# z's products ahead of the gate's in the front of a chunk, and GpSimd's four u ahead of the first scan inputs, with a new merge table

## What is computed

```
xn   = layernorm(x)
z    = xn @ W_in;   gate = silu(xn @ W_gate)
dt   = clip(softplus(z @ W_dt + b_dt), 0.001, 1.0)
Bp   = z @ W_B;     Cp = z @ W_C;   A = -clip(exp(A_log), 1e-6, 1)
h    = exp(dt * A) * h + dt * Bp * z          # step by step over the tokens
y    = sum over states of h * Cp;   out = x + (y * gate) @ W_out
```

## Time and profile before

| what | value |
|---|---|
| median of 3 runs | 3286.13 us (3277.07 to 3286.29) |
| span of the profiled execution | 3287.9 us |
| TensorE busy | 2907.9 us, 88% |
| VectorE busy | 2739.3 us, 83% |
| ScalarE busy | 2096.2 us, 64% |
| GpSimd busy | 1925.7 us, 59% |

### The profile page before, as it was taken

How to read it: one execution, slowest core, us unless ns; L and a number is a source line. 1 busy time by engine, 2 the same in 40 slices (tenths; PEclk the granted TensorE clock), 3 DMA queues, 4 the chain that set the end, 5 groups by cost and what they waited for, 6 DMA issues and landing times.

```text
span 3287.9 us, 45422 instructions
## 1 busy us (share of the span) xinstructions
PE 2907.9 (88%) x14848; PEld 2380.8 (72%) x14848; DVE 2739.3 (83%) x4612; ACT 2096.2 (64%) x3852; POOL 1925.7 (59%) x1541
## 2 busy tenths in 40 slices
PE   6567698998999899898989989899999989998898
PEld 4455477787877778687777868777777877777676
DVE  3777989797998979799898979889897989989541
ACT  2546476676757677675767767576766767575433
POOL 1766667564766757475675756576575647666110
PEclk8558699999999999999999999999999999999998
DMA  4241123231322323232322323232232323223122
GB/s 130 96 159 39 52 81 111 92 102 64 129 82 91 125 78 100 70 118 85 100 103 81 106 79 125 66 106 92 87 109 86 108 76 121 78 71 120 56 103 76
DMA packets 152778, 308.56 MB, mean 94 GB/s; under 512 B 18368, under 2 KB 96984, under 8 KB 135136
## 3 DMA queue, kind: packets, MB, share of 16 engines
q1 hardware_dynamic: 152000, 302.52, 27.6%
q10 hardware_dynamic: 272, 1.57, 0.1%
q0 software_dynamic: 272, 1.57, 0.1%
HBM read 288.27 MB, written 17.35 MB: 93 GB/s over the span
## 4 chain that ended last, share of the span: by engine, by line
PE 48%; DVE 18%; issue 13%; ACT 12%; POOL 5%; DMA 1%; DVEq 0%; SPq 0%; POOLq 0%; ACTq 0%
PE ps_B L1870 11%; PE ps_B L1765 10%; PE ps_A L1765 8%; DVE hs L1527 8%; PE ps_H L1760 7%; DVE acc L1491 5%; PE ps_H L1778 4%; PE ps_B L1760 3%; POOL bu L1100 3%; PE ps_B L1778 3%; PE ps_B L1917 2%; ACT ps_A L1288 2%; DMA bb<-b_rows 1%; DVE hA L1719 1%; ACT acc L1300 1%
## 5 line engine op out<-in xcount | busy, mean ns | idle before, releaser
L1100 POOL TENSOR_TENSOR bu<-z,bb 128x512 f32<-128x512 f32 x1024 | 1294.2, 1290 | 289.9 <-DVE hs L1527 146.7
L1527 DVE TENSOR_TENSOR_SCAN hs<-ps_A,state,bu 128x512 f32<-128x512 f32 x768 | 976.5, 1276 | 21.7 <-ACT ps_A L1288 11.4
L1288 ACT ACTIVATE ps_A<-dt,a_neg 128x512 f32<-128x512 f32 x1024 | 699.3, 686 | 355.7 <-DVE hs L1527 351.5
L1760 PE MATMUL ps_H<-ident,hs 128*128 128x128 f32 x4096 | 652.6, 294 | 195.3 <-DVE acc L1491 123.1
L1760 PEld LDWEIGHTS ps_H<-ident,hs 128*128 128x128 f32 x4096 | 528.3, 151 | 329.2 <-DVE acc L1491 152.0
L1870 PE MATMUL ps_B<-ws_out,hid 128*128 128x256 f32 x2944 | 699.4, 382 | 15.5 <-ACT hid L1437 6.1
L1491 DVE SCALAR_TENSOR_TENSOR acc<-ps_H,ctok,acc 128x512 f32<-128x512 f32 x960 | 700.2, 731 | 8.0 <-PE ps_H L1760 7.1
L1870 PEld LDWEIGHTS ps_B<-ws_out,hid 128*128 128x128 f32 x2944 | 537.0, 191 | 85.1 <-ACT hid L1437 9.9
L1765 PE MATMUL ps_B<-fh,ws_in 128*128 128x512 f32 x1440 | 537.6, 418 | 10.3 <-DVE bl L1680 4.3
L1527 DVE TENSOR_TENSOR_SCAN hs<-ps_A,bu 128x512 f32<-128x512 f32 x256 | 310.9, 1216 | 32.2 <-ACT ps_A L1288 20.0
L1765 PEld LDWEIGHTS ps_B<-fh,ws_in 128*128 128x128 f32 x1440 | 271.0, 188 | 70.5 <-DVE cb L1664 8.1
(11 more groups left out here) (349 smaller groups left out, 4807.7 us busy)
## 6 DMA issues: line engine op xcount, KB each, us to landing
ws_in<-w_split SPq DMA_DIRECT2D x126, 1024.0 KB, 5.4
bb<-b_rows SPq DMA_DIRECT2D x256, 256.0 KB, 3.9
ws_out<-in_L_ffn_V_rwkv SPq DMA_DIRECT2D x64, 512.0 KB, 5.8
ws_out<-in_L_ffn_W SPq DMA_DIRECT2D x32, 512.0 KB, 6.9
xb<-in_L_attn_x SPq DMA_DIRECT2D x16, 512.0 KB, 5.3
n<-in_L_attn_x SPq DMA_DIRECT2D x16, 512.0 KB, 3.9
w_split<-wsp SPq DMA_DIRECT2D x8, 1024.0 KB, 5.6
out<-xb SPq DMA_DIRECT2D x16, 512.0 KB, 3.2
```

The source lines that it names most:

```text
L1100: pool.tensor_tensor(bu[:, u % 4, :], z[:, d, :], bb[:, s % 2, :], ALU.mult)\
L1288: act.activation(b.t[:, :], dt[:, d, :], ACT.Exp, scale=a_neg[:, d, s:s + 1])\
L1527: dve.tensor_tensor_scan(hs[:, s % 2, d, :], b.t[:, :], bu[:, k % 4, :], state[:, s, d:d + 1] if i % CPB else 0.0, ALU.mult, ALU.add)\
L1760: return pe.transpose(dst, src, ident[:, :])
```

## The change

Three things are edited. In FRONT, and in the lists of TensorE and ScalarE, z's four products (and their read-out) come ahead of the gate's. On ScalarE ct and the four logarithms also come ahead of the gate's read-out. On GpSimd the four u are made one after the other, then a new step "bu" waits for the last products and makes the first four bu; before, u and bu alternated. And PACE is made anew for all engines, which moves steps of all lanes.

```diff
-FRONT = ["xn0", "xn1", "bc", "dt0", "dt1", "dt2", "dt3", "gt0", "gt1", "gt2", "gt3", "ct", "z0", "z1", "z2", "z3"]
+FRONT = ["xn0", "xn1", "bc", "dt0", "dt1", "dt2", "dt3", "z0", "z1", "z2", "z3", "ct", "gt0", "gt1", "gt2", "gt3"]
...
                         pool.tensor_tensor(z[:, k, :], z[:, k, :], dt[:, k, :], ALU.mult).then_inc(s_u.sem, 1)
-
-                        if k == 0:
-                            for use in ("gt2", "gt3", "z2", "z3"):
-                                take(pool, i, use)
+                    yield "bu"
+                    for use in ("gt2", "gt3", "z2", "z3"):
+                        take(pool, i, use)
+                    for k in range(DB):
                         pool.wait_ge(s_u.sem, s_u.at(i, k + 1))
                         input_of(i, k)
...
@@ ScalarE: the loop over gate{k} moves from ahead of "ct" to behind the loop over softplus{k};
@@ the loop over z{k} moves from behind "ct" to ahead of it
@@ TensorE: the loops over gate{k} and z{k} change places around "ct"
```

More of the change, by code:

```diff
@@ L168 @@
     "sp": {
[6 rows of a table removed]
-        253, "e1_1": 265, "e1_1_down": 267, "out": 286, "last_mod_x": -26, "last_rv": 161, "last_sw": 172,
-        "last_e0_0": 204, "last_e0_1": 209, "last_e0_0_down": 221, "last_e0_1_down": 232, "last_e1_0": 240,
-        "last_e1_0_down": 277, "last_e1_1": 346, "last_e1_1_down": 346, "last_out": 348,
[8 rows of a table added]
+        "last_out": 361,
     },
     "pool": {
[3 rows of a table removed]
-        152, "rstd_e": 164, "h2": 190, "x_bias": 191, "rstd_h": 214, "rstd_i": 219, "rstd_j": 220, "rstd_m":
-        238, "x5": 286, "last_rstd_e": 169, "last_h2": 170, "last_x_bias": 172, "last_rstd_h": 179,
-        "last_rstd_i": 181, "last_rstd_j": 186, "last_rstd_m": 192, "last_x5": 260,
+        "w_low0": 36, "w_low1": 45, "w_low2": 58, "w_low3": 67, "w_low4": 71, "w_low5": 93, "w_low6": 95, "w_low7":
+        95, "mean0": -30, "rstd0": -25, "h0": -16, "mean1": -12, "rstd1": 9, "gx": 15, "u0": 19, "u1": 19, "u2": 19,
+        "u3": 19, "bu": 19, "xg": 43, "rstd_a": 113, "x_prob": 151, "end_rstd_a": 113, "end_x_prob": 145, "rstd_e":
+        164, "h2": 201, "x_bias": 212, "rstd_h": 214, "rstd_i": 214, "rstd_j": 214, "rstd_m": 240, "x5": 283,
+        "last_rstd_e": 147, "last_h2": 147, "last_x_bias": 149, "last_rstd_h": 156, "last_rstd_i": 156, "last_rstd_j":
+        156, "last_rstd_m": 207, "last_x5": 298,
     },
     "act": {
[21 rows of a table removed]
[20 rows of a table added]
     },
     "dve": {
[5 rows of a table removed]
-        201, "ao1": 204, "h_stats": 204, "h_norm": 206, "i_stats": 208, "i_norm": 208, "j_stats": 209, "lowx0":
[4 rows of a table removed]
-        164, "last_ao1": 165, "last_h_stats": 165, "last_h_norm": 165, "last_i_stats": 173, "last_i_norm": 173,
[4 rows of a table removed]
[14 rows of a table added]
     },
     "pe": {
[27 rows of a table removed]
[25 rows of a table added]
     },
@@ L1251, in n_stream @@
                     for k in range(DB):
-                        yield f"gate{k}"
-                        if i:
-                            used(act, i - 1, f"y{k}")
-                        b = take(act, i, f"gt{k}")
-                        act.activation(gate[:, k, :], b.t[:, :], ACT.Silu, bias=in_col[:, DB + k:DB + k + 1])\
+                        yield f"z{k}"
+                        b = take(act, i, f"z{k}")
+                        act.activation(z[:, k, :], b.t[:, :], ACT.Identity, bias=in_col[:, k:k + 1])\
                            .then_inc(b.free, 1)
@@ L1265, in n_stream @@
                     for k in range(DB):
-                        yield f"z{k}"
-                        b = take(act, i, f"z{k}")
-                        act.activation(z[:, k, :], b.t[:, :], ACT.Identity, bias=in_col[:, k:k + 1])\
-                           .then_inc(b.free, 1)
-                    for k in range(DB):
                         yield f"softplus{k}"
@@ L1273, in n_stream @@
                         act.activation(dt[:, k, :], dt[:, k, :], ACT.Ln, bias=1.0).then_inc(s_dt.sem, 1)
+                    for k in range(DB):
+                        yield f"gate{k}"
+                        if i:
+                            used(act, i - 1, f"y{k}")
+                        b = take(act, i, f"gt{k}")
+                        act.activation(gate[:, k, :], b.t[:, :], ACT.Silu, bias=in_col[:, DB + k:DB + k + 1])\
+                           .then_inc(b.free, 1)
                 def step(i, name, k):
@@ L1798, in n_stream @@
                     for k in range(DB):
-                        yield f"gate{k}"
-                        from_xn(i, f"gt{k}", w_in, DI + k * P)
+                        yield f"z{k}"
+                        from_xn(i, f"z{k}", w_in, k * P)
                     yield "ct"
@@ L1808, in n_stream @@
                     for k in range(DB):
-                        yield f"z{k}"
-                        from_xn(i, f"z{k}", w_in, k * P)
+                        yield f"gate{k}"
+                        from_xn(i, f"gt{k}", w_in, DI + k * P)
                 def step(i, name, k):
```

## The result

The changed kernel takes 3405.72 us (median of 4 runs, 3401.47 to 3410.27) where the kernel before takes 3285.02 beside it: 1.0367 times as long, interval 1.0352 to 1.0381. I had forecast 3276, and 3254 to 3298 as the range. The forecast was wrong in sign and far out of its range.

What follows compares the result with a forecast made beforehand. VectorE was taken to bound the units, the time to the ninth scan each front. 14 chunks x (-0.8 + 0.4) = -5.6 us and chunk 0's -4.1 gave -9.7 on the profiled 3287.9, called 3276; range 3254 to 3298.

Steps and rivals of the forecast that it cites:

- the merge table: Steady chunk's units: its remaining moves fall where VectorE has only 2.7 us idle, so taken as 0.
- The sign that the prediction gave: Units 8 to 63: waits over 0.3 us appearing there would show the forecast wrong.
- The port rival: Front: GpSimd and VectorE block each other at f1l and fl, 1.8 us a chunk, 3301 us; 17%.
- The front's steps: Steady front: chain from last dt exponential to first scan 3.0 us earlier, mostly owed; ninth scan gains 0.8 us.
- VectorE's halt before the first clip: Front: the moved clip waits for the first dt exponential, about 3.5 us, just hidden from nn.
- the 0.47 of fl: Front: one fl lengthened beside GpSimd, 0.47 us added before the ninth scan.
- chunk 0's ninth scan: Chunk 0: freed from GpSimd's alternation, it comes at 107.4 instead of 111.49, a gain of 4.1 us.
- nE's move: Chunk's end: nE starts one decay later, the copy of sm 0.4 us later, a loss of 0.4 us.
- the kept gain: Rival, steady fronts: work moved behind the first scan hides, the 3.0 us stay, 3245 us; 16%.
- a table load less: Rival, ScalarE's fronts: one table serves exponential and logarithm, saving a 1.28 us load, 19 us more, 3257; 3%.

Runs made afterwards that it cites:

- pool_units: New kernel with GpSimd's steps rstd_m, xg, x_prob and x5 back at their old places; 3352.5 us, 1.020 of the kernel before.
- sp_weights2: New kernel with SyncE's loads of the x lane's weights back at their old places; 3328.8 us, 1.013 of the kernel before.
- clear_units2: New kernel with the moves of pool_units and sp_weights2 together, and VectorE's x2 at 158 instead of 151; 3311.6 us, 1.008 of the kernel before.
- u_behind_f1l: clear_units2 with one wait added: from chunk 1 on GpSimd waits for f1l before making u0; 3296.3 us, 1.003 of the kernel before.
- order_only: New code with the old merge table, logarithms just ahead of the gates on ScalarE; 3328.9 us, 1.013 of the kernel before.
- clear_front: clear_units2 with GpSimd's h0 at -25 instead of -16 and f1h ahead of ct and the logarithms on ScalarE; 3418.6 us.

## Why the prediction was wrong

**The step that failed** is the one on the merge table: "The rest of the merge table falls into the stretch that VectorE fills. Its idle time there was 136 - 133.26 = 2.7 us, so no more can come back; I take 0." That bounds the gain and forgets the loss. VectorE's instructions there were taken as fixed durations. They are not: moving GpSimd's and VectorE's steps against each other made them longer, and the stretch from the ninth to the last scan grew by 6.3 us a chunk, 88 us in 14 chunks. pool_units, sp_weights2 and clear_units2 show it, by taking the moves back. The sign that the prediction gave, waits over 0.3 us between units 8 and 63, could not show it: as idle time of VectorE they fell, from 2.5 to 1.7 us a chunk in that stretch.

**The port rival was the right mechanism, at 17%, with the wrong place and size.** I looked for its victims in the front alone, at f1l and fl, and priced 1.8 us. In the front f1l lost 2.1 us of its two and lg 0.3; but the units hold more such instructions (nm_x, choice, x2, hA, and fl), and a table made anew can put any of them beside GpSimd. The Trainium skill, page "SBUF — State Buffer", section "Who interferes with whom", says that a VectorE instruction with two SBUF inputs contends with a GpSimd instruction that reads SBUF, that a tensor-scalar one can contend as well, and that the one issued second waits for the whole of the other. The traces agree: coef 2.27 us for 0.17, wcs<-bmax, a tensor-scalar, 1.14 for 0.17, and lg with its operand in PSUM always 0.19. The prediction had the rule for two inputs only; going through all VectorE instructions with it would have found the kinds that hold 92 of the 122 us (f1l, xb, hA, coef and the second wcs), not the tensor-scalars nm_x and wcs<-bmax, which hold 30.

**The front's steps held but for that.** From the start of the last exponential of dt: z3 at 6.4 us (forecast 6.7), f1h done at 14.4 (14.4), VectorE's halt before the first clip 3.55 us (3.5) and nn without a wait, three table loads, four u in a row. The first scan came at 23.5 (21.0): in chunk 10 f1l's 2.1 and lg's 0.3 make the difference, and in every steady chunk lg's subtraction ends with the fourth bu, a meeting that the prediction didn't list. From the first to the ninth scan 12.3 us, forecast 12.0 and the 0.47 of fl. So the ninth scan came 35.8 us after the last exponential of dt, 1.5 later than before instead of 0.8 earlier. With f1l's wait taken away (u_behind_f1l) it comes at 33.6 in the six chunks at full clock, as forecast (33.5), and at 34.9 in the eight at half clock. So for the front's order the sum came out near (21.6 + 12.0 where it had 21.0 + 12.5); what it lacked there are f1l beside u and the half clock.

**A step was missing.** I followed f1h, f1l and the router's product without TensorE's gate products, which now wait for ScalarE to free their banks behind the logarithms. In the new kernel they end 1.5 us before the delayed f1l in 8 of 14 steady chunks, 0.9 us after it in two, and the first scan comes no later in those; once f1l is short they set the router, as u_behind_f1l and order_only show.

**Right or near:** chunk 0's ninth scan at 109.4 (forecast 107.4, before 111.49), a gain of 2.1 and not 4.1; nE's move cost nothing that shows (from hA's end in unit 59 to the copy of sm 11.0 us before and after; forecast 0.4 more); the kept gain and a table load less did not come.

## What to carry to other kernels

Before a step is moved on either engine, list the VectorE instructions that read two operands from SBUF, and the tensor-scalars on SBUF, and note which GpSimd operation runs at each; in the units here, which VectorE fills, one that met a bu or an xb cost the rest of that operation, however small it was. Idle time doesn't show this: the wait lies in the instruction's duration, so the same form's durations before and after are compared. A halt of GpSimd, for a transfer or for VectorE's own result, is cover for them: a change that removes the halt, or moves either side out of it, has a price although neither engine's work changes. An operand left in PSUM took lg's subtraction out of this.

## What the runs showed of the hardware

Which VectorE instructions wait goes by their kind. In the new kernel, of those that began while GpSimd was at a u, a bu or an xb with 0.35 us or more to go beyond their own time, the tensor-tensors with both operands in SBUF and the tensor-scalars on 128x4 waited (the groups above), while 16 reciprocals took 0.18 us and 104 batch-norm aggregates 0.15, and 63 scalar-tensor-tensors with one operand in PSUM (hA<-ps_B,coef,hA) their usual 0.48.

It also goes by what GpSimd does. Its power of 128x4 numbers, 1.18 us in the profile, didn't delay these: in the new kernel's chunk 10 four scalar-tensor-tensor instructions with SBUF operands run beside it at their usual 0.42 us from start to start (VectorE, then GpSimd). Why is not shown.

```profile
1993.60 1.67 DVE L1471 SCALAR_TENSOR_TENSOR nn<-hA,mv_x,mod_e 128x256 f32<-128x256 f32 x4
...
1993.77 1.18 POOL L1083 TENSOR_TENSOR rs_x<-rs_x,mhalf 128x4 f32<-128x4 f32 x1 [4.85 <-DVE rs_x L1467]
```

A pause of TensorE of 2.6 us (u_behind_f1l) was followed by products at a granted clock of 0.50, 1.2 GHz, with a matmul every 0.43 us instead of 0.23; this came in 8 of its 14 steady chunks, whose first scan is 22.8 us after the last exponential of dt instead of 21.6. After 4.30 and 3.85 us (order_only, clear_front) it came in every one. In the new kernel, with the same pause of 2.6 us, it came in 6 of 14 chunks and cost nothing that shows: lg's subtraction began up to 1.0 us later and ended with the fourth bu all the same.
